# A perceiver block on one core: context rows 13 to a partition, TensorE started in the setup, weights folded earlier

## What is computed

```python
def _L0_xattn_ref(query_input, key_input, value_input, Wq, bq, Wk, bk, Wv, bv):
    q = query_input @ Wq + bq
    k = key_input @ Wk + bk
    v = value_input @ Wv + bv
    attn = jax.nn.softmax(jnp.einsum('bqd,bkd->bqk', q, k) / scale, axis=-1)
    return jnp.einsum('bqk,bkd->bqd', attn, v)
...
x = x + _L0_xattn_ref(_layernorm(x), ctx_1024, ctx_1024, ...)   # ctx_1024: (16, 1601, 256), float32
```

## Time and profile before

| | us |
|---|---|
| median of 3 runs (lowest, highest) | 681.31 (680.92, 681.85) |
| the profiled execution | 680.74 |
| its span, first to last instruction | 679.0 |
| TensorE busy in the span | 611.5 (90%) |
| VectorE, ScalarE, GpSimd busy | 477.6, 364.5, 223.1 |
| moved by DMA | 86.47 MB |

### The profile page before, as it was taken

The page is one execution under the profiler, slowest core; times in us unless marked ns, Lnnn a source line. Parts: engine busy times, 40 slices in busy tenths (PEclk is TensorE's granted clock), DMA queues, the critical chain, the costliest instruction groups (busy, mean ns, idle before and its releaser), DMA issues. The chain is left out here.

```text
span 679.0 us, 11613 instructions
## 1 busy us (share of the span) xinstructions
PE 611.5 (90%) x4390; PEld 458.7 (68%) x4390; DVE 477.6 (70%) x811; ACT 364.5 (54%) x677; POOL 223.1 (33%) x180
## 2 busy tenths in 40 slices
PE   4999998898997777877878999999999999999997
PEld 3455554464335766776767888887787777889897
DVE  3733343347858989999999736678987778876554
ACT  1311111124559898999999643433566456556342
POOL 2000000000004999999989110033553020331000
PEclk9999999999999899999999999999999979999999
DMA  8999999995620222332321000000100022220000
GB/s 315 398 394 389 390 392 390 395 319 170 141 97 31 95 95 94 116 103 96 123 93 63 1 1 1 16 1 17 35 3 3 1 63 77 51 60 1 32 1 31
DMA packets 31182, 86.47 MB, mean 127 GB/s; under 512 B 8012, under 2 KB 19688, under 8 KB 28952
## 3 DMA queue, kind: packets, MB, share of 16 engines
q1 hardware_dynamic: 30984, 85.67, 35.4%
q10 hardware_dynamic: 144, 0.06, 0.1%
HBM read 83.50 MB, written 1.11 MB: 125 GB/s over the span
## 5 line engine op out<-in xcount | busy, mean ns | idle before, releaser
L732 POOL TENSOR_TENSOR dbu<-du,bs 128x1024 f32<-128x1024 f32 x63 | 148.6, 2397 | 206.7 <-DVE du L924 203.9
L946 DVE TENSOR_TENSOR_SCAN w_in<-hS,dbu 128x1024 f32<-128x1024 f32 x42 | 94.8, 2275 | 0.1
L824 ACT ACTIVATE weighed<-T,CT 128x256 f32<-128x256 f32 x220 | 91.2, 543 | 4.3 <-PE T L1028 3.9
L813 ACT ACTIVATE hS<-delta,negA 128x504 f32<-128x504 f32 x128 | 87.3, 757 | 6.7 <-DVE xn L946 4.2
L1042 PE MATMUL Y<-ident,weighed 128*128 128x128 f32 x512 | 67.7, 275 | 0.1
L1028 PE MATMUL T<-ident,w_in 128*128 128x128 f32 x336 | 46.5, 280 | 23.1 <-ACT weighed L824 14.2
L1042 PEld LDWEIGHTS Y<-ident,weighed 128*128 128x128 f32 x512 | 58.7, 142 | 0.8 <-DVE sres L967 0.3
L1028 PEld LDWEIGHTS T<-ident,w_in 128*128 128x128 f32 x336 | 36.2, 141 | 34.0 <-DVE w_in L946 30.4
L946 DVE TENSOR_TENSOR_SCAN xn<-hS,dbu 128x1024 f32<-128x1024 f32 x22 | 50.1, 2279 | 4.8 <-issue 3.3
L297 PE MATMUL O<-cN,pT 128*64 128x256 f32 x384 | 46.7, 385 | 5.0 <-DMA cN<-in_ctx 4.9
L283 PE MATMUL S<-cT,qkT 128*64 128x512 f32 (+1 forms) x256 | 44.8, 502 | 0.8 <-ACT qkT L383 0.8
(11 more groups left out here) (426 smaller groups left out, 1332.8 us busy)
## 6 DMA issues: line engine op xcount, KB each, us to landing
cT<-in_ctxT SPq DMA_DIRECT2D x8, 3202.0 KB, 22.2
cN<-in_ctx SPq DMA_DIRECT2D x8, 3072.0 KB, 23.9
bs<-b_rows SPq DMA_DIRECT2D x32, 512.0 KB, 3.7
raw_w<-in_w SPq DMA_DIRECT2D x16, 256.0 KB, 2.8
w<-in_w SPq DMA_DIRECT2D x7, 256.0 KB, 7.8
vs<-vx SPq DMA_DIRECT2D x8, 136.0 KB, 2.4
x<-in_x SPq DMA_DIRECT2D x2, 512.0 KB, 5.4
cR<-in_ctx SPq DMA_DIRECT2D x8, 128.0 KB
```

Of the source, the lines that this page charges most:

```text
L732: e.tensor_tensor(dbu[s % NB][:, :, :], half(m.du, s // DS), row, ALU.mult).then_inc(s_bu, 1)
L813: i = e.activation(by_batch(A[s % 2][:, j * HALF:(j + 1) * HALF]), by_batch(m.delta[:, c, h * HALF:(h + 1) * HALF]), ACT.Exp, scale=m.negA ...
L824: i = e.activation(weighed[s % 2][:, q * Q:(q + 1) * Q], T[:, q * Q:(q + 1) * Q], ACT.Copy, scale=c_of(s, q))
L946: e.tensor_tensor_scan(S[s % NS], A[s % 2][:, :], dbu[s % NB][:, :, :].rearrange("p c n -> p (c n)"), 0.0, ALU.mult, ALU.add).then_inc(s_h, 1)
```

## The change

Three edits. **Context rows:** `ROWS` becomes 13; 123 partitions (`FULL`) take 13 consecutive rows of each batch, and the 2 rows left go to partition 123 of the same tile. `cR` and its semaphores go. The two transfers of a tile, 123 partitions and one, post to one semaphore. Chunks 0 and 1 have 124 keys, the others 123. **Setup:** TensorE transposes the identity 20 times, in the first block and again 6 and 4 times after it; ScalarE loads its table for the square root there. **Fold:** the product of the weight matrices stands ahead of the first tokens' transposes; ScalarE instead of VectorE copies `wqT`; the bias products follow later.

```diff
-ROWS = LK // P
-MAIN = ROWS * P
-REST = LK - MAIN
+ROWS = LK // P + 1
+FULL = LK // ROWS
+REST = LK - FULL * ROWS
...
-    e.dma_start(k.cN[r][:, :, :, :], k.ctx[2 * i:2 * i + 2, 0:MAIN, :].rearrange("b (p c) d -> p b c d", c=ROWS)
+    e.dma_start(k.cN[r][0:FULL, :, :, :],
+                k.ctx[2 * i:2 * i + 2, 0:FULL * ROWS, :].rearrange("b (p c) d -> p b c d", c=ROWS)
                 ).then_inc(k.s_dN[r], 16)
...
-    for rows in (slice(0, 64), slice(64, REST)):
-        e.dma_start(k.cR[r][rows, :, :], k.ctx[2 * i:2 * i + 2, MAIN + rows.start:MAIN + rows.stop, :].rearrange("b p d -> p b d")
-                    ).then_inc(k.s_dR[r], 16)
+    e.dma_start(k.cN[r][FULL:FULL + 1, :, 0:REST, :], k.ctx[2 * i:2 * i + 2, FULL * ROWS:LK, :].unsqueeze(0)
+                ).then_inc(k.s_dN[r], 16)
...
-            return slice(c, c + (P - 1) * ROWS + 1, ROWS) if c < ROWS else slice(MAIN, LK)
+            return slice(c, c + (n_keys(c) - 1) * ROWS + 1, ROWS)
-            return P if c < ROWS else REST
+            return FULL + 1 if c < REST else FULL
...
+            keep_busy(6)
+            turn_query_weights()
+            keep_busy(4)
+            fold()
             turn_first(0)
-            e.wait_ge(k.s_w0, k.n_w0)
-            fold()
+            fold_query_bias()
             project(0)
...
-                    e.wait_ge(s_dN[(i - 1) % 2], 16 * ((i - 1) // 2 + 1))
+                    e.wait_ge(s_dN[(i - 1) % 2], 32 * ((i - 1) // 2 + 1))
...
+            def keep_turned():
+                e.wait_ge(s_fold, 1)
+                e.activation(wqT[:, :, 0:D], O[:, :].rearrange("p (c n) -> p c n", c=KD), ACT.Copy).then_inc(s_fs, 1)
...
+            @block.tensor
+            def _(e):
+                e.wait_ge(k.s_const, 2)
+                for i in range(20):
+                    e.transpose(busy[:, i % 4 * P:(i % 4 + 1) * P], k.ident[:, :], k.ident[:, :])
...
+                e.activation(root0[:, :], k.ident[:, 0:1], ACT.Sqrt)
```

More of the change, by code:

```diff
@@ L135, in cross_attention @@
         qbk = sb("qbk", [P, TILES])
-        cT, cN, cR, s_dT, s_dN = k.cT, k.cN, k.cR, k.s_dT, k.s_dN
+        cT, cN, s_dT, s_dN = k.cT, k.cN, k.s_dT, k.s_dN
         prob = [sb(f"prob{r}", [P, LK]) for r in range(2)]
-        pT = sb("pT", [P, ROWS + 1, P])
+        pT = sb("pT", [P, ROWS, P])
         mx = sb("mx", [P, 1])
@@ L226, in turn_first, with keep_busy, turn_query_weights @@
                         i.then_inc(s_t0, 1)
-            def fold():
+            def keep_busy(n):
+                for i in range(n):
+                    e.transpose(X[:, i % 4 * P:(i % 4 + 1) * P], k.ident[:, :], k.ident[:, :])
+            def turn_query_weights():
+                e.wait_ge(k.s_w0, k.n_w0)
                 for c in range(KD):
@@ L233, in fold, with fold_query_bias @@
                 i.then_inc(s_fold, 1)
+            def fold():
+                e.wait_ge(s_fs, 1)
+                for r in range(KD):
+                    for c in range(KD):
+                        i = e.matmul(tps[0][:, r * D:(r + 1) * D], wqT[:, c, r * P:(r + 1) * P], k.wk0T[:, c, :],
+                                     start=c == 0, stop=c == 1)
+                i.then_inc(s_fold, 1)
+            def fold_query_bias():
                 for m in range(KD):
@@ L238, in fold, with fold_key_bias @@
                 i.then_inc(s_fold, 1)
+            def fold_key_bias():
                 e.wait_ge(s_fv, 1)
[L240 to L244, removed]
                 for c in range(KD):
@@ L255, in project @@
                     if n == 1:
+                        fold_key_bias()
                         turn_first(1)
+                        e.wait_ge(s_fs, 3)
                     if n >= 2:
@@ L291, in values @@
                     e.wait_ge(s_on, i)
-                if g == 3:
-                    e.wait_ge(k.s_dR[r], 32 * (i // 2 + 1))
                 for c in groups[g]:
                     for b in range(2):
-                        v = cN[r][:, b, c, :] if c < ROWS else cR[r][:, b, :]
-                        j = e.matmul(O[64 * b:64 * b + 64, 0:D], pT[0:n_keys(c), c, 64 * b:64 * b + 64], v,
-                                     start=c == 0, stop=c == ROWS)
+                        j = e.matmul(O[64 * b:64 * b + 64, 0:D], pT[0:n_keys(c), c, 64 * b:64 * b + 64],
+                                     cN[r][0:n_keys(c), b, c, :], start=c == 0, stop=c == ROWS - 1)
                 return j
@@ L372, in _, with keep_bias @@
         def _(e):
+            def keep_turned():
+                e.wait_ge(s_fold, 1)
+                e.activation(wqT[:, :, 0:D], O[:, :].rearrange("p (c n) -> p c n", c=KD), ACT.Copy).then_inc(s_fs, 1)
             def keep_fold():
                 e.wait_ge(s_fold, 2)
+                e.activation(wqk[:, :, :], tps[0][:, :].rearrange("p (c n) -> p c n", c=KD), ACT.Copy).then_inc(s_fs, 1)
+            def keep_bias():
+                e.wait_ge(s_fold, 3)
                 e.activation(qcol, tps[1][:, 0:KD], ACT.Copy).then_inc(s_fs, 1)
-                e.wait_ge(s_fold, 3)
-                e.activation(wqk[:, :, :], tps[0][:, :].rearrange("p (c n) -> p c n", c=KD), ACT.Copy).then_inc(s_fs, 1)
             def move(n):
@@ L381, in move @@
                 e.wait_ge(s_pp, n + 1)
-                e.wait_ge(s_fs, 1)
+                e.wait_ge(s_fs, 3)
                 e.activation(qkT[:, m, h * HALF:(h + 1) * HALF], tps[n % 2][:, :], ACT.Identity, bias=qcol[:, m:m + 1]
@@ L411, in move_first @@
                              bank[n].rearrange("p (u c n) -> p c u n", u=2, c=KD), ACT.Copy).then_inc(s_e0, 1)
+            keep_turned()
             root_first(0)
+            keep_fold()
             move_first(0)
             move_first(1)
-            keep_fold()
+            keep_bias()
             root_first(1)
@@ L469, in _ @@
                     e.wait_ge(k.s_w0, k.n_w0)
[L470 to L472 removed]
+                    e.tensor_copy(wqT[:, :, D], k.cols[:, COLS["bq0"][0]:COLS["bq0"][0] + KD]).then_inc(s_fv, 1)
             e.wait_ge(k.s_bv, 16)
@@ L3005, in perceiver @@
         k.cN = [sb1(f"cN{r}", [P, 2, ROWS, D]) for r in range(2)]
-        k.cR = [sb1(f"cR{r}", [REST, 2, D]) for r in range(2)]
-        k.s_dR = [sem(f"a_dR{r}") for r in range(2)]
         k.w_v0 = t["wv0"]
@@ L3031, in early_loads @@
             e.dma_start(k.b2[:, :], t["b2"]).then_inc(k.s_w6, 16)
-        with nc.Block() as block:
+        with ExitStack() as sctx, nc.Block() as block:
+            sb0, ps0, _ = tools(nc, sctx)
+            busy = ps0("busy")
+            root0 = sb0("root0", [P, 1])
+            @block.tensor
[3 more added lines that the diff above has]
+                    e.transpose(busy[:, i % 4 * P:(i % 4 + 1) * P], k.ident[:, :], k.ident[:, :])
             @block.sync
```

## The result

| | before | after |
|---|---|---|
| median, us (lowest, highest) | 681.12 (678.76, 681.85) | 987.12 (986.33, 989.07) |
| ratio, 95% interval | 1 | 1.450 (1.4472 to 1.4529) |
| span of the profiled execution | 679.0 | 985.8 |
| first scores begin | 23.78 | 18.56 |
| last weighted sum begins | 146.69 | 450.52 |

The change makes the kernel 45% slower. The forecast was 941, with a range up to 985: the direction and the three engines hold, the size misses by 46 us, and the result lies 2 us above the range. What the forecast lacked is a slowdown of transfers beside each other. From the scan's first projection to the end the span is 522.7 us before (679.0 - 156.32) and 523.2 after (985.8 - 462.62), so the whole difference arose in the attention layer.

A forecast was written before the change was run, and what follows sets the result against it. TensorE (15.1 us a tile) and transfers (16.8) almost in balance; `cN` on three engines moves the last weighted sum from 146.69 to 403.1 us (+256.4), plus 3.3 for a slow start: +259.7, 940.4 profiled, median 941, range 915 to 985.

The forecast's parts named there:

- three engines: Attention layer's `cN` transfers: 123 partitions are dealt in equal shares over 3 of 16 DMA engines; chance 0.80, median 941 us.
- Through at 24.0 us: Start of the attention layer: the 8.36 MB queued ahead of the first `cN` are through at 24.0 us.
- 41.2 us for `cN`: Attention layer, each tile: a third of `cN`, 1.092 MB, takes each of the three engines 41.2 us.
- the 1.5 us for the completion: End of the last `cN`: 1.5 us for completion takes the sum from 401.6 to 403.1 us.
- 6 x 7.9 = 47.4 for the six `cT` between: Three engines' queues: each `cT` between the `cN` adds its sixteenth, 7.9 us, 47.4 us for six.
- 15 us less: Lower bound: at 436/16 and 425/16 GB/s an engine, `cN` takes 40.1 and `cT` 7.7 us, giving 926 us.
- rival A: Attention layer: all 16 engines take part, so the start's 5.2 us gain stays; median 676 us (670 to 680), chance 0.13.
- Rival B: Attention layer: all 16 engines, but transfers absorb the 5.2 us gain as waits, no change; 681 us, chance 0.04.
- TensorE's side costs nothing: Attention layer, context rows: 13 chunks with the same columns to stream; 0 taken, 0.3 us a tile as the worst.
- setup and fold: Kernel start: first scores at about 18.6 instead of 23.78, 5.2 us earlier, worth 0 with 3 engines.
- the slow start, +3.3: Last weighted sum, after TensorE idles some 35 us: half pace adds one half of a tile's 6.5 us sum, +3.3.
- such stands will be longer: SP's issue of transfers: its 5.69 us stand will lengthen but end while work is queued, adding nothing.

The follow-up runs named there:

- no_cT: Changed kernel with `cT` loaded for tiles 0 and 1 only, later tiles reusing these: 893.06 us (one run).
- cut112: Changed kernel with its 123-partition `cN` transfer issued as two, 112 and 11 partitions: 763.62, 765.27, 778.21 and 788.57 us.
- all128: Changed kernel with `cN` as one transfer of 128 partitions, 13 rows each at a pitch of 12, no two-row transfer: 681.44 us, ratio 1.0006.
- fold_only: Changed kernel with 12 rows to a partition and `cR` again, so early setup and fold alone: 681.41 us, ratio 0.9997.
- all128_wide_turns: all128 with the transposes reading probabilities at a step of 12 and all chunks 128 keys wide: 675.22 us, ratio 0.9901.
- rows_only: Kernel before with only the edit of the context rows, 13 to a partition, setup and fold as before: 986.08 us, ratio 1.4513.
- wide_only: Kernel before with `cR` loaded as 128 rows in one 128-partition transfer, 65 used, except the last tile: 676.11 us, ratio 0.9923.
- two64: all128 with its `cN` transfer issued as two of 64 partitions each, same pieces: 756.64 us, ratio 1.109.
- cut120: Changed kernel with its 123-partition `cN` transfer issued as two, 120 and 3 partitions: 786.83 us, ratio 1.1565.
- half_hi: Changed kernel, from tile 2 on `cN` to partitions 0 to 50 only and `cT` to 64 to 127 only: 816.04 us (one run).
- half_lo: Changed kernel, from tile 2 on `cN` to partitions 0 to 50 only and `cT` to 0 to 63 only: 824.35 us (one run).

## Why the prediction was right and wrong

**Right: three engines.** "Equal shares over 3 engines" is the share of 0.19 and the rate of 80 GB/s. "Through at 24.0 us" is the fall from 412 to 88 at 24.0. 41.2 us for `cN` is 40.9 in no_cT, whose last sum came at 357.06, where the forecast's own terms without the six `cT` give 403.1 - 47.4 = 355.7. Among these the 1.5 us for the completion comes from no row; in no_cT the first sum, at 67.07, is 1.9 us behind 24.0 + 41.2.

**Wrong: the term "6 x 7.9 = 47.4 for the six `cT` between".** It prices a `cT` by what the three engines themselves carry of it, and takes for granted that the thirteen others, on engines of their own, cost `cN` nothing. Measured, all that is in flight runs at half pace until the thirteen are done, 15.5 us; half of it, 7.8, is lost to `cN`, and the pair of traces gives 15.6 a `cT` in all. With 15.7 in place of 7.9 the forecast's sum becomes 403.1 + 6 x 7.8 = 449.9; measured 450.52. This accounts for the first sum as well: 24.0 + 41.2 + 1.5 is 66.7, and 74.44 was measured, 7.7 later, since the third `cT` runs beside the first `cN`. That the sum comes within 0.6 us is in part luck: the next five gaps add up to 282.3 us where the terms give 284.5, and the last two to 93.8 where they give 90.3, with `w_in` and other loads beside the last `cN`. Carried through, the forecast becomes 680.7 + 303.2 + 3.3 = 987.2 for the profiled execution, which took 987.68. The range's bounds varied the engine's rate by 3 and 8 per cent (the earlier trace rows and the page's mean) and had no case in which transfers slow each other, so that even with the ten us added for other things its upper end stayed 2 us short. (The lower bound's "15 us less" is 10 by its own figures, 8 x 1.1 + 6 x 0.2; nothing hangs on it.) It was also there to be read in part: the earlier trace rows show 390 GB/s and the earlier trace rows 420 at the same share near 1, and the forecast used both without asking what lay between them.

**Wrong, and without effect on the number: rival A's "all 16 engines take part, so the gain of the start stays", 676.** cut112 has all 16 and takes 764 us at best; and all128 with the full rate takes 681.4, as the transposes eat the gain. Rival B, given 0.04, was the better account of the fold: fold_only is at 681.4, with 5.3 us more of waits in place of the 5.2 us.

**Wrong, and hidden: "TensorE's side costs nothing", worst 0.3 us a tile.** It is 1.35. The step counted columns to stream and left out the loads of the transposes, which become 123 and 124 wide. Beside waits of 38 us it costs nothing; in all128 it takes most of the gain: all128_wide_turns, with all loads 128 wide, is at 675.2 where all128 has 681.4.

**Right: setup and fold.** Scores at 18.56 (18.6 forecast), the product's 8 records at 8.68, and no use of it while transfers bound the stage. But the 5.2 us count from 23.78, and that start is slower than others of the same code: in rows_only and wide_only, with setup and fold as before, the product takes 1.97 us in place of 3.76 and the scores begin at 21.62 and 21.67. Against these the two edits are worth 3.1 us.

**Too large: the slow start, +3.3.** The first group of each sum takes 3.4 to 3.7 us instead of 1.95. From the last sum to the projection it is 12.10 us for 9.63, +2.5, of which 0.8 are the transposes of that stretch, so about 1.7 are the slow start. The granted clock stands at 0.50 over the idle stretches, the lower of the two levels (1.2 GHz of 2.4), and is still 0.50 from 450 to 454 us, while the last sum begins.

**SyncE's stands** became 22.8, 23.6 and 25.8 us long in the first issues of `cN`, and 54.1 in the longest, as "such stands will be longer" had it. In the attention layer's windows of 2 us the share falls below 3/16 only to 0.17, mostly where one `cN` ends, so the three engines had work nearly throughout and the stands added nothing that can be seen.

## What to carry to other kernels

Keep every large transfer at 128 partitions, or load surplus rows to get there: 123 cost 306 us here, 64 in a small transfer 5, and the surplus rows cost less than what they gave back. Read GB/s beside the DMA share: a share of 1 at half the rate says that all engines are busy and slow, and in the changed kernel the transfer beside was slowed too. Take windows in which one transfer alone is in flight, as a mean over two hides which of them is slow. Before counting an earlier start as a gain, ask whether the transfers of the stage can start earlier as well.

## What had not been expected of the hardware

- A transfer to 64 partitions goes at half the rate by itself, with all 16 engines busy: 200 GB/s in two64, between `cT` at 412, where all128 has 420. With 112 and 11 partitions it is 218 (cut112), with 120 and 3 it is 202 (cut120).
- Three engines alone run at full pace, 26.7 GB/s each, and a `cT` of 128 partitions alone at 416. Side by side they have 206 together in the changed kernel, at a share near 1, and both are slowed.
- A weight load of 123 or 124 float32 columns of probabilities takes 347 to 361 ns (a step of 13 or 12), one of 128 at a step of 12 takes 223.
- What slows transfers beside each other stays open: half_hi and half_lo came out alike (23.5 and 23.8 us a tile), and both used transfers of 64 partitions. So does which property of the transfer of 112 or 64 partitions makes it slow.
